# An attention and expert block on one core: the last norm with operands in PSUM and ScalarE's root, and the end of attention in another order

## The reference

```
h = layernorm(x) * (1 + ca) + sa
x = x + ga * attention(h)                     # 8 heads of 64, keys and values from a latent of 64
h = layernorm(x) * (1 + cb) + sb
x = x + gb * ffn(h)

ffn(h):  logits = h @ Wr + br; two largest of 8 experts, softmax of the two as weights
         each expert takes its 1280 tokens of largest weight
         y = gelu(h @ W1 + b1) @ W2 + b2, times the weight, added up per token
         out = layernorm(h + y) * gamma + beta
```

## Time and profile before

| | us |
|---|---|
| median of 3 runs | 1345.8 (1345.49 to 1347.42) |
| the profiled execution's own time | 1346.97 |
| its span | 1345.2 |
| TensorE busy | 1151.3 (86%) |
| VectorE busy | 990.3 (74%) |
| ScalarE busy | 746.1 (55%) |
| POOL busy | 948.3 (70%) |

### The profile page before, as it was taken

The page is one execution under the profiler, slowest core; times in us unless marked ns, Lnnn a source line. Parts: engine busy times, 40 slices in busy tenths (PEclk is TensorE's granted clock), DMA queues, the critical chain, the costliest instruction groups (busy, mean ns, idle before and its releaser), DMA issues. The chain is left out here.

```text
span 1345.2 us, 23643 instructions
## 1 busy us (share of the span) xinstructions
PE 1151.3 (86%) x5959; PEld 770.5 (57%) x5960; DVE 990.3 (74%) x2224; ACT 746.1 (55%) x1448; POOL 948.3 (70%) x1086
## 2 busy tenths in 40 slices
PE   7899999999999999999999999999993065989400
PEld 5556566666656566656656566666642045989400
DVE  4888687777777677777777687777675994767596
ACT  4666667666665657666665667565542611444254
POOL 4576978788887969788886969787773205545268
PEclk9899999999999999999999999999995556999755
DMA  5000101010110101020110101010113303233474
GB/s 153 17 19 17 48 18 64 2 64 17 48 47 16 48 16 63 0 63 15 48 47 16 47 16 48 2 49 1 48 48 126 78 1 97 45 95 48 101 251 163
DMA packets 68478, 70.91 MB, mean 53 GB/s; under 512 B 12912, under 2 KB 64032, under 8 KB 68272
## 3 DMA queue, kind: packets, MB, share of 16 engines
q1 hardware_dynamic: 46800, 47.18, 11.0%
q10 hardware_dynamic: 16896, 16.78, 3.7%
q0 software_dynamic: 4704, 6.11, 3.0%
HBM read 40.35 MB, written 29.45 MB: 52 GB/s over the span
## 5 line engine op out<-in xcount | busy, mean ns | idle before, releaser
L705 ACT ACTIVATE PF<-PS 128x512 f32<-128x512 f32 x512 | 298.5, 595 | 256.9 <-PE PS L1087 248.8
L979 DVE TENSOR_REDUCE NMAX<-PS 128x1 f32<-128x512 f32 x512 | 342.5, 682 | 88.5 <-PE PS L1096 85.0
L567 POOL TENSOR_TENSOR SF<-SF,PF 128x512 f32<-128x512 f32 x252 | 323.1, 1303 | 14.0 <-ACT PF L705 13.8
L1168 PE MATMUL PS<-PF,V 128*64 128x512 f32 x1024 | 248.0, 605 | 0.0
L1086 PE MATMUL PS<-Q,K 128*128 128x512 f32 x512 | 221.9, 433 | 2.8 <-ACT PF L705 2.8
L1096 PE MATMUL PS<-K,Q 128*128 128x512 f32 x512 | 205.7, 403 | 10.4 <-DVE NMAX L979 10.2
L1087 PE MATMUL PS<-Q,K 128*128 128x512 f32 x512 | 201.5, 394 | 0.0
L724 ACT ACTIVATE Q<-PS 64x512 fp32r<-64x512 f32 x256 | 151.7, 593 | 48.2 <-PE PS L172 43.3
L644 POOL TENSOR_TENSOR XL<-XF,XH 128x512 fp32r<-128x512 f32 x63 | 83.1, 1320 | 128.2 <-ACT XH L779 128.2
L1086 PEld LDWEIGHTS PS<-Q,K 128*128 128x128 f32 x512 | 96.4, 188 | 120.3 <-issue 55.2
L564 POOL TENSOR_TENSOR SF<-PF 128x512 f32<-128x512 f32 x126 | 162.4, 1305 | 3.9 <-ACT PF L705 3.4
(11 more groups left out here) (351 smaller groups left out, 2449.3 us busy)
## 6 DMA issues: line engine op xcount, KB each, us to landing
X<-in_L_attn_x SPq DMA_DIRECT2D x16, 512.0 KB, 3.5
MODB<-mod_rows SPq DMA_DIRECT2D x16, 512.0 KB, 3.7
h_rows<-H ACTq DMA_DIRECT2D x16, 512.0 KB, 3.0
acc_rows<-H ACTq DMA_DIRECT2D x16, 512.0 KB, 4.1
out_x<-X SPq DMA_DIRECT2D x16, 512.0 KB, 2.9
A<-acc_rows SPq DMA_DIRECT2D x15, 512.0 KB, 8.9
W1F<-in_L_ffn_W SPq DMA_DIRECT2D x3, 1024.0 KB
W2F<-in_L_ffn_W SPq DMA_DIRECT2D x3, 1024.0 KB, 7.4
```

The lines of the kernel that those rows point to most:

```text
L567: s_sum.done(pool.tensor_tensor(total, total, tile, ALU.add))
L705: s_exp.done(act.activation(PF[:, u % 8, :], st_bank(u), ACT.Exp))
L979: s_mred.done(dve.tensor_reduce(NMAX[:, p % 2, r:r + 1], mx_bank(u), AX.X, ALU.max, negate=True))
L1168: last = pe.matmul(num_bank(p)[odd * R:(odd + 1) * R, :], V1[:, vp, c, :], PF[:, k % 8, :], start=(c == 0), stop=(c == TC - 1))
```

## The change

In attention:
- The early choice's 20 steps are done in units 12 to 31 of the last batch, one each, where 13 of them were in units 19 to 31 and seven in the four units behind. Its exponential moves from unit 28 to 21.
- For the last batch the norm is done in halves of two row blocks. VectorE aggregates after the second and after the fourth block. POOL does two operations per half (variance plus epsilon, power), and VectorE the other four (`final_scale`), both halves after the fourth block's statistics. ScalarE waits for a half each.

In the last norm:
- The steps are 13 in place of ten. Five of their tiles (`TMP`, `ODD`, `DEL2`, `SUM`, `Y2`) lie in PSUM bank 7, and no step has two sources in SBUF; the three steps more are a copy, a second difference and a product. The normalised pairs go round seven banks.
- POOL's power is gone, and its constant. ScalarE makes the square root (`root`), for group 0 ahead and for group j+1 in the middle of group j, and VectorE the reciprocal.

```diff
@@ -305,7 +305,7 @@
-    TOP_AT, TOP_EXP = [(NB - 1, 19 + k) for k in range(13)] + [(NB, k // 2) for k in range(7)], (NB - 1, 28)
+    TOP_AT, TOP_EXP = [(NB - 1, 12 + k) for k in range(20)], (NB - 1, 21)
@@ -329,6 +329,8 @@
     s_norm = S("norm", NORM_OPS)
+    FINAL_OPS = 6
+    s_fnorm = [sem(f"fnorm{j}") for j in range(2)]
@@ -520,6 +522,16 @@
 
                 new, old = exists(b + 2), exists(b - 1)
                 if not (new or old):
+                    return
+                if final(b - 1):
+                    for j in range(2):
+                        cols = slice(TC + 2 * j, TC + 2 * j + 2)
+                        s_stat[1].wait(pool, b - 1, TC * j + TC - 1)
+                        if j == 0:
+                            s_xn2.wait(pool, b - 2, TC - 1)
+                        pool.tensor_tensor(NV[:, cols], MV[:, cols, 1], EPSC[:, cols], ALU.add).then_inc(s_fnorm[j], 1)
+                        pool.wait_ge(s_fnorm[j], 1)
+                        pool.tensor_tensor(NY[:, cols], NV[:, cols], HALF[:, cols], ALU.pow).then_inc(s_fnorm[j], 1)
@@ -764,7 +776,10 @@
-                        s_norm.wait(act, scale_of(pb + 1), NORM_OPS - 1)
+                        if final(pb):
+                            act.wait_ge(s_fnorm[c // 2], FINAL_OPS)
+                        else:
+                            s_norm.wait(act, scale_of(pb + 1), NORM_OPS - 1)
@@ -793,11 +808,30 @@
-                if c == TC - 1:
+                if which and final(nb):
+                    if c % 2:
+                        st.wait(dve, nb, c + c // 2 * 2)
+                        gate(which, TC)
+                        for k in range(TC + c - 1, TC + c + 1):
+                            st.done(dve.bn_aggr(MV[:, k, :], NS6[:, k, :]))
+                elif c == TC - 1:
                     st.wait(dve, nb, c)
                     gate(which, TC)
                     for k in range(which * TC, (which + 1) * TC):
                         st.done(dve.bn_aggr(MV[:, k, :], NS6[:, k, :]))
+
+            def final_scale(j):
+
+                cols, done = slice(TC + 2 * j, TC + 2 * j + 2), s_fnorm[j]
+                v, y, t, nmr, mean = NV[:, cols], NY[:, cols], NTMP[:, cols], NB1[:, cols], MV[:, cols, 0]
+                dve.wait_ge(done, 2)
+                dve.tensor_tensor(t, y, y, ALU.mult).then_inc(done, 1)
+                dve.wait_ge(done, 3)
+                dve.scalar_tensor_tensor(out=t, in0=t, scalar=-0.5, in1=v, op0=ALU.mult, op1=ALU.mult).then_inc(done, 1)
+                dve.wait_ge(done, 4)
+                dve.scalar_tensor_tensor(out=y, in0=t, scalar=1.5, in1=y, op0=ALU.add, op1=ALU.mult).then_inc(done, 1)
+                dve.wait_ge(done, 5)
+                dve.scalar_tensor_tensor(out=nmr, in0=mean, scalar=-1.0, in1=y, op0=ALU.mult, op1=ALU.mult).then_inc(done, 1)
@@ -957,6 +991,9 @@
                             norm_stats(1, jb, idx)
+                            if final(jb) and idx == TC - 1:
+                                for j in range(2):
+                                    final_scale(j)
@@ -1862,15 +1899,15 @@
-    STEPS, VAR_DONE, PAIRS, BANKS = 10, 6, NCH // 2, 8
+    STEPS, VAR_DONE, PAIRS, BANKS = 13, 8, NCH // 2, 7
-    VAR, DEL, SUM, Y, TMP, NMR = (sb(x, [P, NCH]) for x in ("VAR", "DELt", "SUMt", "Yr", "TMP", "NMR"))
-    GATE, HALF = sb("GATEt", [P, NB]), sb("HALFt", [P, NCH])
-
-    s_half = sem("thalf")
+    VAR, DEL, Y, NMR = (sb(x, [P, NCH]) for x in ("VAR", "DELt", "Yr", "NMR"))
+    TMP, ODD, DEL2, SUM, Y2 = (PS[:, BANKS, j * NCH:(j + 1) * NCH] for j in range(5))
+    GATE, ROOT = sb("GATEt", [P, NB]), sb("ROOTt", [P, NCH])
-    s_pow, s_gate, s_stat, s_step, s_xn, s_mul, s_add, s_out = (sem(x) for x in ("tpow", "tgate", "tstat", "tstep", "txn", "tmul", "tadd", "tout"))
+    s_root, s_gate, s_stat, s_step, s_xn, s_mul, s_add, s_out = (sem(x) for x in ("troot", "tgate", "tstat", "tstep", "txn", "tmul", "tadd", "tout"))
@@ -1911,36 +1948,50 @@
+            v, d, t, y, s, nmr, odd, d2, y2 = (x[:, cols] for x in (VAR, DEL, TMP, Y, SUM, NMR, ODD, DEL2, Y2))
+
+            def made(i):
+
+                dve.wait_ge(s_step, STEPS * j + i + 1)
+
...
             if k == 0:
                 dve.wait_ge(s_stat, FIRST[j + 1])
+                ins = dve.tensor_copy(odd, mean_o)
             elif k == 1:
+                ins = dve.tensor_scalar(t, m2_e, 1.0 / D, EPS, ALU.mult, ALU.add)
             elif k == 2:
+                made(0)
+                ins = dve.tensor_tensor(d, mean_e, odd, ALU.subtract)
             elif k == 3:
+                ins = dve.tensor_tensor(d2, mean_e, odd, ALU.subtract)
             elif k == 4:
+                made(1)
+                ins = dve.scalar_tensor_tensor(out=v, in0=m2_o, scalar=1.0 / D, in1=t, op0=ALU.mult, op1=ALU.add)
             elif k == 5:
+                made(3)
+                ins = dve.scalar_tensor_tensor(out=d2, in0=d2, scalar=0.25, in1=d, op0=ALU.mult, op1=ALU.mult)
             elif k == 6:
+                ins = dve.tensor_tensor(s, mean_e, odd, ALU.add)
             elif k == 7:
+                made(5)
+                ins = dve.tensor_tensor(v, d2, v, ALU.add)
             elif k == 8:
+                dve.wait_ge(s_root, j + 1)
+                ins = dve.reciprocal(y2, ROOT[:, cols])
             elif k == 9:
+                made(8)
+                ins = dve.tensor_tensor(d, v, y2, ALU.mult)
+            elif k == 10:
+                made(9)
+                ins = dve.scalar_tensor_tensor(out=d, in0=d, scalar=-0.5, in1=y2, op0=ALU.mult, op1=ALU.mult)
+            elif k == 11:
+                made(10)
+                ins = dve.scalar_tensor_tensor(out=y, in0=d, scalar=1.5, in1=y2, op0=ALU.add, op1=ALU.mult)
+            elif k == 12:
+                made(11)
+                ins = dve.scalar_tensor_tensor(out=nmr, in0=s, scalar=-0.5, in1=y, op0=ALU.mult, op1=ALU.mult)
+            ins.then_inc(s_step, 1)
@@ -1973,9 +2024,18 @@
+        def root(j):
+
+            cols = slice(FIRST[j], FIRST[j + 1])
+            act.wait_ge(s_step, STEPS * j + VAR_DONE)
+            act.activation(ROOT[:, cols], VAR[:, cols], ACT.Sqrt).then_inc(s_root, 1)
+
+        root(0)
         for j in range(len(GROUPS)):
             act.wait_ge(s_step, STEPS * (j + 1))
             for c in range(FIRST[j], FIRST[j + 1]):
+                if j + 1 < len(GROUPS) and c == (FIRST[j] + FIRST[j + 1]) // 2:
+                    root(j + 1)
@@ -1983,20 +2043,7 @@
-        pool.memset(HALF[:, :], -0.5).then_inc(s_half, 1)
-        pool.wait_ge(s_half, 1)
-
-        def power(j):
-
-            cols = slice(FIRST[j], FIRST[j + 1])
-            pool.wait_ge(s_step, STEPS * j + VAR_DONE)
-            pool.tensor_tensor(Y[:, cols], VAR[:, cols], HALF[:, cols], ALU.pow).then_inc(s_pow, 1)
-
-        power(0)
         for q in range(PAIRS):
-            for j in range(1, len(GROUPS)):
-                if 2 * q == FIRST[j - 1]:
-                    power(j)
```

More of the change, by code:

```diff
@@ L1919, in step @@
             elif k == 1:
-                dve.tensor_tensor(d, mean_e, mean_o, ALU.subtract).then_inc(s_step, 1)
+                ins = dve.tensor_scalar(t, m2_e, 1.0 / D, EPS, ALU.mult, ALU.add)
             elif k == 2:
-                dve.wait_ge(s_step, STEPS * j + 1)
-                dve.scalar_tensor_tensor(out=v, in0=m2_o, scalar=1.0 / D, in1=t, op0=ALU.mult, op1=ALU.add).then_inc(s_step, 1)
+                made(0)
+                ins = dve.tensor_tensor(d, mean_e, odd, ALU.subtract)
@@ L1937, in step @@
-                dve.scalar_tensor_tensor(out=t, in0=t, scalar=-0.5, in1=v, op0=ALU.mult, op1=ALU.mult).then_inc(s_step, 1)
+                made(5)
+                ins = dve.tensor_tensor(v, d2, v, ALU.add)
             elif k == 8:
-                dve.wait_ge(s_step, STEPS * j + 8)
-                dve.scalar_tensor_tensor(out=y, in0=t, scalar=1.5, in1=y, op0=ALU.add, op1=ALU.mult).then_inc(s_step, 1)
+                dve.wait_ge(s_root, j + 1)
+                ins = dve.reciprocal(y2, ROOT[:, cols])
```

12 lines of the change are left out of this document (removed).

## The result

The changed kernel takes **1331.3 us** (median of 4 runs, 1330.6 to 1332.1), against 1346.6 us for the kernel before in the same comparison (4 runs, 1345.5 to 1348.5). The ratio is 0.9887, with a 95% interval of 0.9874 to 0.9899. The forecast was 1331.5 us, as a gain of 14.3 us on 1345.8; the gain is 15.3 us, on a kernel before that was 0.8 us slower in this comparison. The profiled execution took 1331.5 us, with a span of 1329.8.

A forecast was written before the change was run, and what follows sets the result against it. POOL's adds bound the last norm, and a chain across engines the end of attention. Last norm -13.0 and attention's end -1.3 give -14.3 us, from 1345.8 to 1331.5 us; range 1328 to 1338.

The forecast's parts named there:

- Last norm, -13.0 predicted: Last norm: without POOL's powers and with unheld VectorE steps, POOL's adds end at 1328.1 against 1341.14, -13.0 us.
- The first round: VectorE's last-norm loop of statistics, steps and products: the round gains three steps, +0.3 us, ending at 1281.85.
- The last 20 adds: End of last norm: POOL's adds form a solid run from 1303.6, 1.225 us each, to 1328.1.
- The price of a PSUM operand: VectorE's last-norm steps with a PSUM side: 0.10 us of pitch each, without the skill page's higher fixed cost.
- The time by that page, 1334.0: Last norm: with 120 cycles for PSUM against 58, 39 steps cost 65 ns more each, 2.5 us; time 1334.0.
- steps still held: Last norm: VectorE's steps stretch as before, only the powers go, -6.8 us there, 1337.7 in all; 15%.
- Covers: Last norm: ScalarE's roots, table load and seven banks cost nothing; VectorE ends about 4 us ahead of POOL.
- The hole in TensorE, 2.5 us predicted: End of attention: early steps delay YT of block 2, TensorE idles 2.5 us near 977; last pair +0.9 us.
- the early choice is hidden: End of attention: VectorE catches up, nothing moves by 2.8 us; that part gives -4.1, time 1328.7; 10%.
- The norm in halves, -2.2 predicted: Last batch of attention: ScalarE's four H end at 1022.0 against 1024.15, -2.2 us.
- the sum of this part: End of attention: +0.9 us for the moved choice and -2.2 for the halves, together -1.3 us.
- the clock falls: At the new TensorE hole near 976 the clock falls and stays low, +29 us, 1360 in all; 3%.

The follow-up runs named there:

- tiles in SBUF: The changed kernel with TMP, ODD, DEL2, SUM and Y2 of the last norm in SBUF, ScalarE's root and 13 steps kept: 1346.3 us, ratio 0.9994 to the kernel before.
- the second (1332.2): The changed kernel itself measured once more, unmodified, beside other kernels on the same chip: 1332.2 us, ratio 0.9900 to the kernel before.
- the halves alone: The kernel before with only the last batch's norm in halves, early choice and last norm as before: one execution, attention's end 64.89 us.
- the late choice: The changed kernel with the early choice back at its old places (13 steps in units 19 to 31, seven behind): 1330.6 us, ratio 0.9886 to before.
- spread, two adds moved: The changed kernel with the choice's 20 steps in units 19 to 31 and the last norm's last two adds on VectorE: 1327.5 us, ratio 0.9850 to before.

## Why the prediction was right, point by point

- **Last norm, -13.0 predicted, -13.6 measured.** The chain of steps in it held too. The first round was to grow by 0.3 us for its three more steps and grew by 0.05. The two that follow were to take 9.1 and 11.5 us and took 8.8 and 11.2 (10.8 and 14.4 before). The first product of group 2 was to be done 1.1 us after the last of these and was done after 1.3 (1300.39 + 0.69). The last 20 adds were to start 33.5 us after the first statistics (1303.6 on the clock of the kernel before) and started after 32.9; they were to take 1.225 us each and took 1.226. So the 0.6 us lies in the rounds: 0.10 us per step was a little too much, as 0.08 fits them better. It is also less than the 0.9 us by which the stage scatters from profile to profile.
- **The price of a PSUM operand.** Where nothing holds them, the steps but for the reciprocal take 0.14 to 0.18 us with a PSUM side and 0.15 to 0.18 with SBUF alone, but for one of 0.24. L1978, which reads PSUM, takes 0.155 to 0.174 for 16 columns, and the same step from SBUF, in the run with the tiles there, 0.158 to 0.174; L1962 into PSUM and L1963 into SBUF take 0.16 each. The Trainium skill's page "VectorE: DVE Perf Modes", section on the TRN2 errata, has twice the fixed cost for PSUM sources; for steps of 8 and 16 columns this trace does not show it, and the measurement decides. The time by that page, 1334.0, was 2.7 us too long.
- **Rival "steps still held", 15%.** It did not come: no step of the 65 is over 0.24 us. The Trainium skill, "SBUF — State Buffer", section Who interferes with whom, says that VectorE and GpSimd block each other when VectorE has two SBUF inputs or a 2-port mode; the runs agree in both directions, PSUM sides free the steps (0.16) and SBUF ones hold them (1.10), a one-operand copy among them. But **the rival's price was wrong**. The prediction kept the first product of group 2 at its old time and took away only the powers, -6.8 us. The run with the tiles in SBUF, in which steps are held as the rival has it, shows nothing gained. The failed step is "and only the powers go" with the 24.5 us behind it: it put the last 20 adds at POOL's pace, where in fact the held steps let VectorE set the pace there too, and the adds took 30.3 us. The product ahead of them, 39.7 us after the first statistics by the rival, was done after 40.7.
- **Covers.** The roots, the table load (1.28 us) and the seventh bank cost nothing, as said. VectorE was to end 4 us ahead of POOL and ends 4.6 ahead.
- **The hole in TensorE, 2.5 us predicted.** It is there, 0.61 + 1.74 = 2.35 us, in two pieces. YT of block 2 moved by 2.62 (2.4 predicted), the router's product by 2.83 (2.8), the last transpose by 0.76 (0.9). The rival "the early choice is hidden" did not come.
- **The norm in halves, -2.2 predicted.** Where the clock does not differ it gave -1.9 and -2.1 at the last H; alone -1.5, with 0.4 lost to the clock. The size was right, the parts less so. The first half's power took 0.98 us and the second's 0.69, where "0.7 for two" columns was said; the second half's L832 took 0.58 beside POOL, where a step was put at 0.22, and tore a gap of 0.55 us into ScalarE's four H. The aggregates ahead of block 2's YT cost 0.28 us (1.53 between the YTs of blocks 1 and 2, against 1.25 before), where 0.2 was said.
- **Why the sum of this part held** (-1.3 predicted at the last H, -1.5 measured). The last pair started 0.76 us later (0.9 predicted). The aggregates added 0.28. From YT of row block 3 to the last H the changed kernel takes 5.02 us against 7.21, -2.2. That makes -1.15, and the clock gave back the rest: TensorE was busy with the delayed products up to the last pair, so the idle time of 2 us ahead of it that the earlier trace rows show was gone. The granted clock stayed at 1.00 up to 52.16 us after the first cut, to the end of block 3's projection, where it had fallen at 49.13 before. From that projection to its YT it takes 0.78 us against 1.10. The forecast had no such term, so that the sum came out this near is in part luck.
- **Rival "the clock falls", 3%.** Its first half happened, in most executions; its second half did not. The clock does fall at this hole in five profiles of seven, but it is back at 1.00 after 3.4 us (three profiles) or 6.8 (two), while TensorE went on working. The price was not 29 us: 0.7, 1.0 and 1.1 us at attention's end in the three profiles whose code up to there is that of the changed kernel. The failed condition is "and stayed low". With the price right, the case belonged into the forecast's own sum, at 0.7 to 1.1 us in most executions, and not among the rivals.

The first comparison of the changed kernel (1331.3) hit the forecast of 1331.5 to 0.2 us, the second (1332.2) to 0.7. That is better than the parts deserve. The kernel gained 15.3 us where 14.3 was forecast, and the comparison's kernel before was 0.8 us slower (1346.6) than the 1345.8 that the forecast started from: the two nearly cancel. By the stages of the two profiles the last norm gave 0.6 us more than said and attention's end 0.3 more, and the stretches with the same code move by more than that by themselves.

## What to carry to other kernels

Two engines that share operands' memory can bind each other in turn: a short VectorE step that is held until POOL's current add ends costs up to that add's length, and POOL pays it back by waiting for what stands behind the step. Where one shows 0.15 us alone and 1.1 beside POOL, count the held steps per product first; taking work off POOL gains nothing as long as they are there, and the two edits belong together (0 and 4.6 us apart, 13.6 together).

A step moved "earlier, where it is hidden" is hidden only if the engine has idle time ahead of its next deadline, not on average. Here the choice, moved up to clear one wait, made a hole in TensorE 30 us further up, which cost 0.4 us more than the wait gave and 1.1 where the clock fell.

Once one engine is a solid run of equal instructions to the end, its count is the time: move some of them to the engine that has finished.

## What the runs showed of the hardware

- A POOL power costs by column and is dear at any width: 128x2 took 0.69 and 0.98 us, 128x8 1.64 to 1.68, 128x16 2.91. ScalarE's root of 128x16 takes 0.22 and VectorE's reciprocal 0.24.
- The granted clock is not a property of the program alone. Idle times of 0.61 and 1.74 us with one matmul between them ended in a fall to 0.50 in five profiles of seven, and the clock was back at 1.00 after 3.4 or 6.8 us. A single idle time of 2.0 us before the last pair went either way: the clock fell right behind it in the halves alone (first matmul 0.55 us), not so in the changed kernel with the late choice, where the matmuls behind it took 0.36 and 0.28 and the fall came 1.8 us after their start. And a single idle time of 1.4 to 1.65 us near 22 us after the first cut left the clock at 1.00 in six kernels and was followed by 3.4 us at 0.50 in a seventh (spread, two adds moved), whose matmul there takes 0.77 us and not 0.47:

```profile
987.17 0.77 PE L1123 MATMUL PS<-Q,K 128*128 128x512 f32 x1 [1.43 <-ACT PF L717]
```

- VectorE and POOL in turn, above: all 42 steps that took over 0.3 us, in the last norm of the kernel before and of that with the tiles in SBUF, end 0.02 to 0.04 us after one of POOL's adds. VectorE's own add of 128x512 in "spread, two adds moved" waited for two of POOL's adds.
